# Tile scores of the router: from two TensorE products to row sums on ScalarE, GpSimd and VectorE

## The reference, cut to what matters

```python
xf = xn.reshape(N, D)                                   # the normed row, D = 512
slope_sign = jnp.sign(jnp.mean(spline_slopes, axis=-1)) # one sign for each column
tile_sigs = zeros((64, D)).at[tile, its 8 columns].set(slope_sign)
cluster_sigs = jnp.sign(tile_sigs.reshape(8, 8, D).mean(axis=1))
input_sigs = jnp.sign(xf)
best_cluster = jnp.argmax(input_sigs @ cluster_sigs.T, axis=-1)
tile_scores = input_sigs @ tile_sigs.T
tile_idx = argmax of tile_scores within best_cluster
```

## Time and profile before

| what | before |
|---|---|
| runs | 8645.66, 8651.39, 8653.18 us |
| the profiled execution | 8648.8 us |
| its span, first to last instruction | 8647.0 us |
| busy: PE, DVE, POOL, ACT, of the span | 88%, 77%, 66%, 54% |
| mean granted TensorE clock over the span | 0.942 |
| `core_phase`, roughly | from 7070 to 8425 us of the span |

### The profile page before, as it was taken

One profiled execution on the slowest core, in us unless ns is written; L12 is line 12 of the kernel. 1 busy time (PEld: TensorE's weight loads), 2 busy tenths in 40 slices (PEclk: granted clock), 3 DMA queues, 4 the chain that ended last, 5 costly groups with the idle time before them and its releaser, 6 DMA issues. The chain is left out here.

```text
span 8647.0 us, 222908 instructions
## 1 busy us (share of the span) xinstructions
PE 7638.4 (88%) x76550; PEld 5615.1 (65%) x76550; DVE 6621.9 (77%) x8318; ACT 4702.7 (54%) x10584; POOL 5670.5 (66%) x3272
## 2 busy tenths in 40 slices
PE   5659999999989989989999999899999989999984
PEld 3337777777777777777777777644444436666653
DVE  4439999999999999999999999622222237878776
ACT  4447777777777777777777787511111112222220
POOL 0009999999999999999999999600000015554544
PEclk8779999999999999999999999999999988988885
DMA  3350000000000000000000000121221222222215
GB/s 134 137 158 0 20 21 0 20 21 1 19 21 20 0 21 20 0 21 20 8 13 20 20 0 5 60 83 68 87 82 68 92 79 78 76 79 74 79 66 168
DMA packets 198786, 423.53 MB, mean 49 GB/s; under 512 B 22448, under 2 KB 48496, under 8 KB 183024
## 3 DMA queue, kind: packets, MB, share of 16 engines
q1 hardware_dynamic: 172768, 382.77, 13.2%
q10 hardware_dynamic: 25872, 38.80, 1.2%
HBM read 225.11 MB, written 196.41 MB: 49 GB/s over the span
## 5 line engine op out<-in xcount | busy, mean ns | idle before, releaser
L485 POOL TENSOR_TENSOR scan_hc<-scan_h,scan_cb 128x1024 f32<-128x1024 f32 x2048 | 4776.9, 2366 | 265.8 <-DMA scan_cb<-scratch_bc 127.5
L651 DVE TENSOR_TENSOR_SCAN scan_h<-scan_a,scan_carry,scan_u 128x512 f32<-128x512 f32 x4096 | 4802.1, 1260 | 156.0 <-PE scan_u L590 128.1
L590 PE MATMUL scan_u<-scan_dg,scan_v 64*128 64x128 f32 x32768 | 2391.7, 286 | 339.1 <-DVE scan_h L651 280.1
L536 ACT ACTIVATE scan_a<-scan_dt,scan_aneg 128x512 f32<-128x512 f32 x4096 | 2659.9, 708 | 44.8 <-issue 30.5
L590 PEld LDWEIGHTS scan_u<-scan_dg,scan_v 64*128 64x128 f32 x32768 | 2000.7, 188 | 819.1 <-DVE scan_h L651 538.0
L598 PE MATMUL scan_y<-scan_ident,scan_hc 128*128 128x128 f32 x16408 | 2251.0, 280 | 60.1 <-POOL scan_hc L485 33.6
L598 PEld LDWEIGHTS scan_y<-scan_ident,scan_hc 128*128 128x128 f32 x16408 | 1764.8, 141 | 310.3 <-POOL scan_hc L485 34.5
L507 ACT ACTIVATE scan_dg<-scan_half,scan_bt 128x64 f32<-128x64 f32 x4096 | 1139.2, 341 | 5.0 <-DVE scan_onward L634 5.0
L528 ACT ACTIVATE scan_carry<-scan_h,scan_onward 128x4 f32 (+1 forms) x1008 | 303.0, 301 | 1042.5 <-DVE scan_h L651 1042.5
L177 POOL TENSOR_TENSOR mid_r<-mid_ve,mid_half_neg 128x4 f32<-128x4 f32 x32 | 32.4, 1012 | 1271.4 <-DVE mid_ve L132 784.1
L1141 POOL TENSOR_TENSOR core_joint<-core_own 128x32 f32<-128x32 f32 x64 | 17.4, 272 | 621.2 <-DVE core_own L1271 536.6
(11 more groups left out here) (211 smaller groups left out, 7647.3 us busy)
## 6 DMA issues: line engine op xcount, KB each, us to landing
scratch_y<-scan_yo ACTq DMA_DIRECT2D x17, 1024.0 KB, 4.7
pre_x<-in_x SPq DMA_DIRECT2D x16, 1024.0 KB, 6.8
scratch_z<-pre_zt SPq DMA_DIRECT2D x16, 1024.0 KB, 3.9
scratch_dt<-pre_dt SPq DMA_DIRECT2D x16, 1024.0 KB, 4.6
scratch_vr<-pre_vr ACTq DMA_DIRECT2D x16, 1024.0 KB, 4.7
scan_dt<-scratch_dt SPq DMA_DIRECT2D x16, 1024.0 KB, 5.3
scan_v<-scratch_vr SPq DMA_DIRECT2D x32, 512.0 KB, 7.8
scan_z<-scratch_z SPq DMA_DIRECT2D x16, 1024.0 KB, 10.7
```

Source lines behind the costliest of these rows:

```text
L485: pool.tensor_tensor(hc[:, q].rearrange("p n (r j) -> p n r j", j=P), h[:, q].rearrange("p n (r j) -> p n r j", j=P), cb[:, bass.ds(b * NS ...
L536: ins = act.activation(a[:, q, n, :], dt[:, par, q, :], ACT.Exp, scale=aneg[:, q, bass.ds(m * 2 + n, 1)])
L590: mm = pe.matmul(u_ps[:, q % 2, g, k * HP:(k + 1) * HP, :], v[row, par, k, q, :], dg[row, buf, k], start=True, stop=True)
L651: ins = dve.tensor_tensor_scan(h[:, q, n, :], a[:, q, n, :], u_ps[:, q % 2, :, :, n].rearrange("p g t -> p (g t)"), carry[:, q, bass.ds(m ...
```

## The change

`turn_x` and `tile_scores` leave TensorE. ScalarE takes the sign of xf row by row, from SBUF to the new tile `sg`. GpSimd multiplies `sg` in place by `sgn`, slope_sign written along every row (`flip`, lead 1, between `totals` and `keys`). VectorE sums each 8 columns to `ts`, each 8 tiles to `cl`, joins them (`both` = 512 cl + ts) and makes the key = 64 both + key_row. `route` moves from behind `spread_scores` to ahead of it. `sgn` is made once ahead of the loop by four products of a tile of ones with `diag` (the identity times slope_sign), copied from PSUM by ScalarE; the load of `key_pattern` goes. `products` no longer waits for the key, and `turn_keys` waits for ScalarE's third copy of the item before in place of its sign of two items before.

```diff
-        S_STATE, S_X3, S_VE, S_KEEP, S_XF, S_OH = 1, 2, 5, 10, 12, 14
+        S_STATE, S_X3, S_VE, S_KEEP, S_XF, S_OH = 1, 2, 5, 10, 12, 17
...
             pool.wait_ge(zeroed, 10)
+            pool.wait_ge(sgn_ready, 1)
...
+            def flip(i, par, m):
+
+                act_r.wait(pool, i, 2)
+                pool_b.inc(pool.tensor_tensor(sg[:], sg[:], sgn[:], ALU.mult))
...
-            pipelined(pool, ITEMS, [(1, root), (3, totals), (4, keys), (1, pick), (4, more_keys)])
+            pipelined(pool, ITEMS, [(1, root), (3, totals), (1, flip), (4, keys), (1, pick), (4, more_keys)])
...
-                dve.tensor_scalar(tiles[:, q, :], pattern[:, q, :], slope_sign[:, q:q + 1], None, ALU.mult).then_inc(tiles_ready, 1)
+                dve.tensor_scalar(diag[:, q, :], ident[:], slope_sign[:, q:q + 1], None, ALU.mult).then_inc(tiles_ready, 1)
...
             def route(i, par, m):
...
-                pe_r.wait(dve, i, 2)
-                dve.tensor_tensor(key[:], sc_ps[:, 1, 0:NT], key_row[:], ALU.add).then_inc(key_read, 1)
-                dve.wait_ge(key_read, i + 4)
+                pool_b.wait(dve, i, 2)
+                dve.tensor_reduce(ts[:], sg[:].rearrange("p (n e) -> p n e", e=8), AX.X, ALU.add).then_inc(key_read, 1)
+                dve.wait_ge(key_read, i + 2)
+                by_cluster = lambda t: t[:].rearrange("p (c n) -> p c n", n=8)
+                after.link(dve, dve.tensor_reduce(cl[:], by_cluster(ts), AX.X, ALU.add))
+                after.link(dve, dve.scalar_tensor_tensor(out=by_cluster(both), in0=cl[:].rearrange("p (c n) -> p c n", n=1).broadcast_to([P, NT // 8, 8]), scalar=512.0, in1=by_cluster(ts), op0=ALU.mult, op1=ALU.add))
+                after.link(dve, dve.scalar_tensor_tensor(out=key[:], in0=both[:], scalar=64.0, in1=key_row[:], op0=ALU.mult, op1=ALU.add))
...
-            pipelined(dve, ITEMS, [(1, state), (1, norms), (0, limits), (1, centred), (4, decays), (3, spread_scores), (1, route)])
+            pipelined(dve, ITEMS, [(1, state), (1, norms), (0, limits), (1, centred), (4, decays), (1, route), (3, spread_scores)])
...
+            act.wait_ge(sgn_made, 1)
+            act.copy(sgn[:], y_ps[:]).then_inc(sgn_ready, 1)
...
             def signs(i, par, m):
 
-                pe_r.wait(act, i, 1)
-                act_r.inc(act.activation(sgt[:], kt_ps[:], ACT.Sign))
+                after.wait(act, i, S_XF)
+                act.wait_ge(key_read, i + 1)
+                act_r.inc(act.activation(sg[:], xf[:], ACT.Sign))
...
+            for q in range(Q):
+                mm = pe.matmul(y_ps[:, q * P:(q + 1) * P], ones[:], diag[:, q, :], start=True, stop=True)
+            mm.then_inc(sgn_made, 1)
+            pe.wait_ge(sgn_ready, 1)
...
                 pool_a.wait(pe, i, A_KEYS)
-                act_r.wait(pe, i - 2, 2)
+                act_a.wait(pe, i - 1, 3)
...
                 spread.wait_before(pe, i)
-                pe.wait_ge(key_read, i + 1)
                 chain.wait_all(pe, i)
...
-            pipelined(pe, ITEMS, [(2, tree), (2, turn_keys), (3, products), (1, turn_x), (2, reads), (3, turn_scores), (1, tile_scores), (2, sums), (2, outputs)])
+            pipelined(pe, ITEMS, [(2, tree), (2, turn_keys), (3, products), (2, reads), (3, turn_scores), (2, sums), (2, outputs)])
```

More of the change, by code:

```diff
@@ L964, in pipelined, with core_phase @@
         turn((items - tail) // 2 + k // 2, k % 2, tail - 1 - k)
-def core_phase(nc, D, H, L, a_s, k_s, r_s, v_s, x2_s, wo_d, gam_d, bet_d, slopes_d, key_row_d, key_pattern_d, mask_d, hmask_d, ident_d, x3_s, oh_out, xs_out, ext_out):
+def core_phase(nc, D, H, L, a_s, k_s, r_s, v_s, x2_s, wo_d, gam_d, bet_d, slopes_d, key_row_d, mask_d, hmask_d, ident_d, x3_s, oh_out, xs_out, ext_out):
     B = 2
@@ L1003, in core_phase @@
         ot = sb("ot", [P, Q, P]); s = sb("s", [P, 2, Q, P])
-        x3 = sb("x3", [P, D]); xo = sb("xo", [P, 2, D]); xf = sb("xf", [P, D]); sgt = sb("sgt", [P, Q, P]); pr = sb("pr", [P, D])
+        x3 = sb("x3", [P, D]); xo = sb("xo", [P, 2, D]); xf = sb("xf", [P, D]); sg = sb("sg", [P, D]); pr = sb("pr", [P, D])
         wo = sb("wo", [P, Q, D]); gam = sb("gam", [P, D]); bet = sb("bet", [P, D])
         NT = D // 8
-        key_row = sb("key_row", [P, NT]); pattern = sb("pattern", [P, Q, NT]); tiles = sb("tiles", [P, Q, NT])
+        key_row = sb("key_row", [P, NT]); sgn = sb("sgn", [P, D]); diag = sb("diag", [P, Q, P]); ones = sb("ones", [P, P])
         mask = sb("mask", [P, P]); hmask = sb("hmask", [P, P]); ident = sb("ident", [P, P]); heads = sb("heads", [P, 2, P // 8])
@@ L1010, in core_phase @@
         eps_mul = sb("eps_mul", [P, 2]); eps_add = sb("eps_add", [P, 2]); keep = sb("keep", [P, 2])
-        key = sb("key", [P, NT]); kmax = sb("kmax", [P, 1]); pen = sb("pen", [P, NT]); mm2 = sb("mm2", [P, 2])
+        ts = sb("ts", [P, NT]); cl = sb("cl", [P, NT // 8]); both = sb("both", [P, NT]); key = sb("key", [P, NT]); kmax = sb("kmax", [P, 1]); pen = sb("pen", [P, NT]); mm2 = sb("mm2", [P, 2])
         oh = sb("oh", [P, ITEMS, NT]); xs = sb("xs", [P, ITEMS, 8]); ext = sb("ext", [P, 2, NT])
@@ L1016, in core_phase @@
         consts = sem("consts"); ticks_dve = sem("ticks_dve"); ticks_pool = sem("ticks_pool"); ticks_sp = sem("ticks_sp"); ticks_pe = sem("ticks_pe")
[L1017 removed]
+        pool_ready = sem("pool_ready"); slope_sum = sem("slope_sum"); slope_signs = sem("slope_signs"); tiles_ready = sem("tiles_ready"); zeroed = sem("zeroed"); opened = sem("opened"); key_read = sem("key_read"); sgn_made = sem("sgn_made"); sgn_ready = sem("sgn_ready")
         ins_a = [sem(f"ins_a{i}") for i in range(2)]
@@ L1043, in core_phase @@
         act_a = Count(sem("act_a"), 4)
-        after = Count(sem("after"), 15)
-        S_STATE, S_X3, S_VE, S_KEEP, S_XF, S_OH = 1, 2, 5, 10, 12, 14
-        pool_b = Count(sem("pool_b"), 2)
+        after = Count(sem("after"), 18)
+        S_STATE, S_X3, S_VE, S_KEEP, S_XF, S_OH = 1, 2, 5, 10, 12, 17
+        pool_b = Count(sem("pool_b"), 3)
         routed = Count(sem("routed"), 5)
-        pe_r = Count(sem("pe_r"), 2)
         act_r = Count(sem("act_r"), 2)
@@ L1080, in _ @@
         def _(sp):
-            for dst, src in ((wo, wo_d), (gam, gam_d.partition_broadcast(P)), (bet, bet_d.partition_broadcast(P)), (key_row, key_row_d), (pattern, key_pattern_d), (mask, mask_d),
+            for dst, src in ((wo, wo_d), (gam, gam_d.partition_broadcast(P)), (bet, bet_d.partition_broadcast(P)), (key_row, key_row_d), (mask, mask_d),
                              (hmask, hmask_d), (ident, ident_d)):
@@ L1202, in _ @@
             routed.start(dve)
-            dve.sem_inc(key_read, 3)
+            dve.sem_inc(key_read, 1)
             for t, value in ((kz, 0.0), (rk, 0.0), (s, 0.0), (ext, -BIG), (own, 1.0), (eps_mul, 1.0), (eps_add, EPS)):
@@ L1208, in _ @@
             last.then_inc(zeroed, 1)
+            dve.memset(ones[:], 1.0)
             dve.memset(rr[:, SUB - 1, SUB], 1.0).then_inc(zeroed, 1)
@@ L1213, in _ @@
             dve.wait_ge(zeroed, 10)
-            dve.wait_ge(consts, 144)
+            dve.wait_ge(consts, 128)
             dve.tensor_reduce(slope_sign[:], slopes[:], AX.X, ALU.add).then_inc(slope_sum, 1)
@@ L1375, in _ @@
             pe_b.start(pe)
-            pe_r.start(pe)
-            pe.wait_ge(consts, 144)
+            pe.wait_ge(consts, 128)
             pe.wait_ge(zeroed, 10)
@@ L1432, in products @@
                     pe_a.inc(mm)
[L1434 to L1441, removed]
             def reads(i, par, m):
@@ L1462, in turn_scores @@
                 pe_a.inc(mm)
[L1464 to L1469, removed]
             def sums(i, par, m):
@@ L1666, in program @@
             ln_scale, ln_bias, wx, ww, bw, wk, wv, wr, wo, gamma, beta, slopes, table,
-            ident, half_ident, key_row, key_pattern, sub_mask, head_mask, grid, out):
+            ident, half_ident, key_row, sub_mask, head_mask, grid, out):
     B, L, D = x.shape
@@ L1697, in program @@
     mid_phase(nc, NCH, D, x_rows, y_s, out_proj, ffn_w, ffn_b, ln_scale, ln_bias, wx, ww, bw, wk, wr, wv, ident, x2_s, a_s, k_s, r_s, vv_s)
-    core_phase(nc, D, HEADS, L, a_s, k_s, r_s, vv_s, x2_s, wo, gamma, beta, slopes, key_row, key_pattern, sub_mask, head_mask, ident, x3_s, oh_s, xs_s, ext_s)
+    core_phase(nc, D, HEADS, L, a_s, k_s, r_s, vv_s, x2_s, wo, gamma, beta, slopes, key_row, sub_mask, head_mask, ident, x3_s, oh_s, xs_s, ext_s)
     final_phase(nc, D, N, x3_s, oh_s, xs_s, ext_s, table, grid, ident, out.rearrange("b l d -> (b l) d"))
@@ L1748 @@
         "key_row": const(-1.0 * _np.arange(NT) - 2048.0 * (_np.arange(NT) // SL)),
-        "key_pattern": rows(_np.float32(64.0) * (d // SL == n) + _np.float32(32768.0) * (d // (SL * SL) == n // SL)),
         "sub_mask": (p[:, None] // SUB == p[None] // SUB).astype(_np.float32),
```

1 line of the change is left out of this document (removed).

## The result

The kernel after takes 8706.27 us (median of 4 runs, 8702.61 to 8708.52) beside 8650.39 us for the kernel before in the same batch (4 runs): a ratio of 1.0065, 95% interval 1.0047 to 1.0082. It is slower by 0.65%, 56 us, where the forecast was 8684, 33 us slower than 8651.39. The direction and the range (8630 to 8745) held; the size was short by 22 us.

A forecast was written before the change was run, and what follows sets the result against it. A POOL and DVE ring of 19.77 us was taken to bound the loop; adding 0.60 and 0.87 gave 21.24 a turn, +42 us over 60 turns, -10 behind the loop: +32, 8684 us, range 8630 to 8745.

The forecast's parts named there:

- The ring: Loop turn: own, kc, pick, ql, root on POOL, then tmp, xf, decays on DVE, 19.77 us without a gap.
- PE's late turns: Loop turns where x3 waits for PE's output projection, up to 23.12 us; 0.77 us a turn in the mean.
- the two new costs: Loop: 0.60 us a turn for pick starting later plus 0.87 for the flip, 1.47 expected together.
- DVE's own sum: DVE's work per loop turn after the change: 20.8 us, just under the ring.
- The flip's price: GpSimd's new product beside DVE's decays: 1.09 less 0.20, taken as 0.87 us a turn; ends 0 and 1.3.
- One or two decays 0.9 us longer beside the flip: Sign in the loop's DVE timeline that would show the forecast right.
- Pick's delay: Loop: both and key held up by kc and qr, so pick starts 0.6 us later; ends 0 and 1.2.
- The set-up: Ahead of the loop: four products and ACT's copy, once, cost about nothing; ends 0 and 3 us.
- The tail: Unrolled turns behind the last own: PE's relief wins 10 us; ends 0 and -15.
- Neither cost arises: Rival: POOL and DVE don't lock in the loop, turn stays 19.77 us, 8595 us; chance 0.09.
- one cost arises: Rival: only the flip's cost or only pick's delay in the loop, 8631 or 8647 us; chance 0.15.
- PE's clock: Rival: idling lowers PE's clock until PE bounds the loop; turn 22.1 us, 8735 in one case; chance 0.20.

The follow-up runs named there:

- x4: Changed kernel without GpSimd's sign multiplication and with the first four steps of more_keys ahead of pick: 8612.69 us, ratio 0.9953.
- y2: Kernel before, only order changed: TensorE's turn_x behind turn_scores and tile_scores behind sums, ScalarE's sign behind outputs: 8600.32 us, ratio 0.9938.
- x1: Changed kernel without GpSimd's flip, the multiplication by slope_sign left out: 8634.22 us, ratio 0.9980.
- x2: Changed kernel with the first four steps of more_keys moved ahead of pick on GpSimd: 8682.03 us, ratio 1.0031.
- x3: Changed kernel with ScalarE's copy of sgn moved behind its first copy of the diagonal: 8695.91 us, ratio 1.0050.
- w1: Changed kernel with the flip replaced by a GpSimd memset of the same size in the same place, multiplication left out: 8634.62 us, ratio 0.9980.

## Why the prediction was right, and where it was short

**The ring and PE's share: right.** That a turn is 19.77 us through POOL and DVE, that PE is no part of it, and that PE's late turns cost 0.77 us which any relief of PE wins, was borne out from both sides: 19.91 in x4 without the two new costs, and 19.77 in nearly every turn of y2 with PE's old work. DVE's own sum, worked out at 20.8 us, is 21.44 less the wait of 0.61 for root, 20.83.

**The flip's price: right in kind, too small.** The prediction took 1.09 us, pick's length, less 0.20 = 0.87. The flip takes 1.26 to 1.28 us where no decay runs beside it, in the last three items: not pick's time but that of kl and ql. All of these are products of 128x512, so the size alone doesn't price them; why pick is the shorter one no run tried (its mask is read 8 times per element in a row, kl and ql read a row of 64 elements 8 times over, and the flip reads two full tiles). 1.27 less the 0.20 of the earlier trace rows is 1.07, which is what a decay loses, and `own` loses 1.10; x1 and x4 make it 1.18 and 1.12 on the turn. By x1, which differs from after in the flip alone, the term was short by 0.31 us a turn, 19 us. Of the bounds that were kept, 0 and 1.3, it came out near the upper one.

**How the flip costs: half right.** "One or two decays 0.9 us longer beside the flip" was seen in about a third of the turns, with one decay 1.07 us longer. In the others no decay is longer: the flip is locked out, 7.3 us from its start to its end at the most, and `own` pays (40 of 61 times). That own-to-own would be nearly even was wrong for this reason alone.

**Pick's delay: right, somewhat too large.** Forecast 0.60; in x1, without the flip, the wait is 0.47 and the turn 20.26 us, 0.49 above the ring's 19.77, so 0.11 us a turn, 7 us, were charged too much. The step that was too large is the end of `both` and `key`: 0.14 us behind kc and qr each in the prediction, 0.07 and 0.08 in the trace. `both` looks hardly stretched (0.30) because it starts only 0.23 us ahead of kc's end. What x2 and x4 give back, 0.41 and 0.35, is less than 0.49, since their order has the price told above.

So the turn is 19.77 + 0.49 + 1.18 = 21.44, where the forecast had 19.77 + 0.60 + 0.87 = 21.24, and the loop cost 54 us, not 42. Of the 12 us between, the flip makes 19 and pick -7.

**The set-up: wrong.** "Four set-up products and ACT's copy ... cost about nothing, ends 0 and 3": the head is 8.5 us longer and x3 got 10.4 back. The four products are short indeed, 1.19 us; the failing step was that nobody asked what stands ahead of them on PE (the other opening products) and what stands behind the copy on ACT: the copy of the diagonal, on which the first decays hang.

**The tail: right.** -10 forecast, -8.5 measured.

So the forecast's +32 becomes, with 12 more in the loop, 8.5 at the head and 1.5 in the tail, +54, against 55.9 between the medians. That it was no further off owes 7 us to luck: pick's error has the other sign.

**The rivals.** "Neither cost arises" and "one cost arises" fell: both costs are there. x1 shows what the latter would have been, 8634 (8631 was worked out). "PE's clock" fell too, though the granted clock did go down, from 0.89 to 0.83 over the loop: PE still waits for spread_scores in each of the 55 turns looked at, 4.7 us in the mean, so the lower clock is paid from idle time. That is the "settles near the edge" of the prediction, well inside it. The Trainium skill (TensorE: Matmul & The Clock Gate, What's actually happening) says that idling throttles the clock and activity releases it. By this rule the trace agrees: in the turn shown PE idles 4.1 us up to 7840.23, and the clock granted between its two levels, 1.2 and 2.4 GHz, is 0.68 from 7838.90 to 7844.30 and 1.00 from there to 7856.00.

**The lock.** w1 shows that a GpSimd product that reads SBUF stops VectorE's products and that a memset of the same size, which only writes, does not. The Trainium skill (SBUF — State Buffer, Who interferes with whom) says the same: two SBUF inputs contend with a GpSimd instruction that reads, not with one that only writes. It also says that a copy on VectorE can enter a mode that takes both ports and so contend too. By that the trace agrees: `own`, a copy with one input, was stopped for 1.10 us.

**What stays open.** Ahead of the loop VectorE and GpSimd take turns, while in the turn shown the decays keep GpSimd out for all 12 products that are left of the run. Of the 61 flips that meet decays 21 got in. All 21 had started 0.09 to 0.12 us ahead of the same decay, the first one of 256 columns. Of the 40 that were locked out 23 had started 0.04 to 0.05 us ahead of that decay, and 17 elsewhere in the run, two of them 0.11 us ahead of a decay. So the lead alone doesn't decide who wins. What does, and why GpSimd gets no turn for the rest of the run, is open; no run tried to shift the flip.

## What to carry to other kernels

A GpSimd step that reads SBUF and is put "beside" a run of VectorE products with two SBUF inputs isn't hidden: here it cost VectorE nearly its own length, wherever it landed. Price it by the GpSimd row that reads its operands in the same way, not by any row of the same size, and compare it with doing the step on VectorE, which here cost a third. Before taking work off an engine that looks like the bound, see whether it waits for something in mid-turn: moving the two pieces within PE's list, and the sign within ACT's, won 51 us, more than any form of removing them that was run here. And for one-time work, look at what stands ahead of it and behind it in the queues, not only at how long it is.

## What the runs showed that was not expected

- Back-to-back VectorE products shut a GpSimd instruction out for up to 6 us, not for one instruction: the flip's 1.26 us became a median of 7.04.
- A VectorE copy of 64 elements with one SBUF input took 1.32 us in place of 0.22 beside the flip; with a memset or nothing in its place it never took over 0.22.
- Steps of two elements, 0.16 us each, took 1.20 to 1.23 beside kl and ql: the lock's price went by the GpSimd instruction's length, not the VectorE step's.
- A GpSimd memset of 128x512 takes 0.53 us and hinders none of the decays beside it.
